# A four-layer graph network on one core: the mean of h from one product for four graphs, spread over the partitions by DMA

## The chip, the cores and the metric

The kernel runs on one core of one Trainium2 chip. The metric is the device time of one execution in microseconds (us), the median over runs of the same program. The engines are named as in the profile: PE is TensorE's matrix product, PEld its weight load, DVE is VectorE, ACT is ScalarE, POOL is GpSimd, and SP is SyncE, which here only issues DMAs.

## The reference

Sixteen graphs of 512 nodes with 128 features pass through four layers; each layer is a residual with a layer norm. The first three are attention layers with a dense 0/1 adjacency matrix. The first and the third take the softmax over a row:

```python
def layer0(x, adj_matrix, W, a):
    h = jnp.einsum('bnd,od->bno', x, W)
    e = (h @ a_left)[:, :, None] + (h @ a_right)[:, None, :]
    e = jnp.where(e > 0, e, LEAKY_SLOPE * e)
    e = jnp.where(adj_matrix == 0, NEG_INF, e)
    alpha = jax.nn.softmax(e, axis=-1)
    return jnp.einsum('bij,bjd->bid', alpha, h)
...
x = _layernorm(x + layer0(x, adj, ...), axis=-1)
x = _layernorm(x + layer1(x, adj, ...), axis=-1)   # softmax over the columns, then elu
x = _layernorm(x + layer2(x, adj, ...), axis=-1)   # as layer 0, with a bias in h, then elu
x = _layernorm(x + layer3(x, adj, ...), axis=-1)   # products with the relation masks
```

A row without an edge has all its scores at NEG_INF, so its softmax is uniform and its result is the mean of h over all 512 nodes. The kernel computes that mean for every graph of layers 0 and 2, and adds it in rows that are found to be empty.

## The kernel before, in words

All data stays in SBUF: X holds the 16 graphs (128 partitions, 4 chunks of 128 rows, 128 features), MT the masks. A work item is one graph in one layer; items 0 to 15 are layer 0, 16 to 31 layer 1, 32 to 47 layer 2, 48 to 63 layer 3. Every engine runs the same loop over slots n (`pipeline`), written out by hand: in slot n it treats the items at(-3) to at(4), that is n-3 to n+4, in an order fixed per engine, and waits for semaphores counted per item. No scheduler moves anything.

In slot n of layers 0 and 2:

- PE (from L495): transposes x of item n+4 into `xT_ps` (L416), spreads the column maximum of item n+2 (L459, `smax_ps`), spreads the row factors of item n+1 (L478), projects item n+3 (L437, `h_ps`; in layer 2 first two products that put the bias there, L432 and L434), multiplies the sum of x over the nodes, the same in every column, with the weights (L441, `h_mean_ps`, 128 x 128, so that the mean stands in every partition), and then attends for item n (L491).
- ACT (from L743): the node factors of item n+2, the scaled output of item n-3 (L706), then `take_h` of item n+3: `h_mean` out of PSUM (L643) and `hx` (L645); then xT of item n+4 (L634), with the sum of x over the nodes as accumulator output `x_sum`; in layer 0 also a check of the mask (L733).
- DVE (from L1033): sums of item n-1, the maximum of item n+2 (L897), then the output of item n-2 in layer 0 (y, L994) or of item n-1 in layer 2 (`lin`, which shares its space with `residual`, L994), then layer 2's elu (L1008) and the moments of item n-2, the weights PT of item n+1 (L942), and its own maximum of item n+3 (L892).
- POOL (from L306): scales h of item n+1 (L262). In layer 0 then `mean` of item n-1 (L238: `mean_term` = mean of h times the flag of empty rows) and the residual x + mean_term (L248). In layer 2 `mean` of item n+1, then the elu part of item n-1 (L287). Then 1/sqrt(variance) of item n-2 (L269, L272). In slots -4 to 7 POOL also issues the load of a mask (L225).
- SP: loads x graph by graph (L182), from graph 4 on held back until mask n-3 has landed, then the weights and bias of layer 3, then waits for the outputs (L195).

So in layer 0 the mean of item i is used by DVE in slot i+2 by way of the residual, in layer 2 in slot i+1 by `lin` itself. `mean_term` has two buffers. DVE's L994 waits for POOL's product, and POOL's product for ACT's `h_mean`.

Of the kernel before, what the change touches and what calls it, by code (L numbers as in the profile page):

```python
# [9 lines left out]
ACT = mybir.ActivationFunctionType  # L10
AX = mybir.AxisListType

P = 128
G = 16
N = 512
D = 128
# [17 lines left out]
class Item:  # L34


    def __init__(self, l, g, r):
        self.l, self.g, self.r, self.b, self.m = l, g, r % 4, r % 2, g % 8
        self.done = g + (G * l + 1)
        self.of_layer = g + 1  # L40


def item(n):
    return Item(n // G, n % G, n % G) if n >= 0 else None


def build(nc, x, adj, adj_rows, w_in, w_out, a_in, b2, ab2, w3, b3, out):
    ctx = ExitStack()
    with ctx:
        def sb(name, shape, dt=F32):  # L50
            return ctx.enter_context(nc.sbuf_tensor(name, shape, dt))
# [6 lines left out]
        def sem(name):  # L58
            if name not in sems:
                sems[name] = ctx.enter_context(nc.semaphore(name))  # L60
            return sems[name]


        X = sb("X", [P, G, C, D])
# [5 lines left out]
        empty_col = sb("empty_col", [P, G, C])  # L70
        x_cur = sb("x_cur", [P, C, D])
        xT = sb("xT", [P, 2, N])
        x_sum = sb("x_sum", [P, 2])
        hx = sb("hx", [P, 4, C, 132])
        h_mean = sb("h_mean", [P, 8, D])
        h_scaled = sb("h_scaled", [P, 2, C, 132])
# [35 lines left out]
        wx = sb("wx", [P, 3, 130])  # L112
# [24 lines left out]
        o_ps = [pb(f"o_ps{b}", [P, C, 256]) for b in range(2)]  # L137
        h_all_ps = h_ps[:, :, 0:260].rearrange("p k (c w) -> p k c w", c=2)
        smax_ps, h_mean_ps = h_ps[:, 0, 260:260 + P], h_ps[:, 1, 260:260 + D]

        def h_chunk_ps(c, width):

# [21 lines left out]
        def halves(it):  # L164

            return it.of_layer + (G if it.l == 2 else 0)
# [11 lines left out]
        @block.sync  # L178
        def _(sp):

            def load_x(it):
                sp.dma_start(X[:, it.g, :, :], x[it.g, :, :, :]).then_inc(sem(f"x_in{it.g}"), 16)  # L182

            for n in range(G):
                if n >= 4:

                    sp.wait_ge(sem(f"mask_in{n - 3}"), 16)
                load_x(item(n))
            sp.dma_start(w_rel[:, :, :], w3.rearrange("r d o -> d r o")).then_inc(sem("w_late"), 16)
            sp.dma_start(bias3[:, :], b3.partition_broadcast(P)).then_inc(sem("w_late"), 16)  # L190

            for n in range(G * LAYERS, G * (LAYERS + 1)):
                it = item(n)
                sp.wait_ge(sem("x_new"), it.done)
                sp.dma_start(out[it.g, :, :, :], X[:, it.g, :, :]).then_inc(sem("out"), 16)  # L195
            sp.wait_ge(sem("out"), 16 * G)

            with sp.If(not_binary(sp)):
                with sp.Fori(0, G) as g:
                    settle(sp)  # L200

                    sp.wait_ge(sem("re_adj_free"), g + 1)
                    sp.dma_start(adj_in[:, :, :], adj[g, :, :, :]).then_inc(sem("re_in"), 16)
                    sp.dma_start(X[:, g, :, :], x[g, :, :, :]).then_inc(sem("re_in"), 16)
                    sp.wait_ge(sem("re_x"), g * (LAYERS + 1) + (LAYERS + 1))
                    sp.dma_start(out[g, :, :, :], X[:, g, :, :]).then_inc(sem("re_out"), 16)
                sp.wait_ge(sem("re_out"), 16 * G)
# [4 lines left out]
        def _(pool):  # L212
# [14 lines left out]
            def mean(it):  # L227

                if it.l == 2:
                    if it.g >= 2:  # L230

                        pool.wait_ge(sem("y_lin"), it.of_layer - 2)
                elif it.g >= 2:
                    pool.wait_ge(sem("residual"), it.done - 2)
                pool.wait_ge(sem("h_mean"), halves(it))
                if it.l == 0:
                    pool.wait_ge(sem("empty_row"), it.of_layer)
                pool.tensor_tensor(mean_term[:, it.b, :, :],  # L238
                                   h_mean[:, it.m, :].unsqueeze(1).broadcast_to([P, C, D]),
                                   empty_row[:, it.g, :].unsqueeze(2).broadcast_to([P, C, D]),  # L240
                                   ALU.mult).then_inc(sem("mean_raw"), 1)

            def add_residual(it):
                if it.g >= 2:
                    pool.wait_ge(sem("y_sum"), it.done - 2)
                pool.wait_ge(sem(f"x_in{it.g}"), 16)
                pool.wait_ge(sem("mean_raw"), it.done)
                pool.tensor_tensor(residual[:, it.b, :, :], X[:, it.g, :, :], mean_term[:, it.b, :, :],  # L248
                                   ALU.add).then_inc(sem("residual"), 1)
# [56 lines left out]
            def attention_slot(at, n):  # L306
                if at(8) and at(8).l == 0:
                    load_mask(at(8))
                if at(1) and at(1).l != 1:
                    scale_h(at(1))  # L310
                if at(-1) and at(-1).l == 1:
                    elu_low(at(-1))
                if at(-1) and at(-1).l == 0:
                    mean(at(-1))
                    add_residual(at(-1))
                if at(1) and at(1).l == 2:
                    mean(at(1))
                if at(-1) and at(-1).l == 2:
                    elu_low(at(-1))
                if at(-2):  # L320
                    find_rstd(at(-2))
                if at(1) and at(1).l == 1:
                    scale_h(at(1))
                if n == G + 8:
                    split_bias2()
# [78 lines left out]
        def _(pe):  # L404
# [14 lines left out]
            def next_transpose(it):  # L419
                if it.l > 0 or it.g >= 1:  # L420

                    pe.wait_ge(sem("xT"), it.done - 1)
                if it.l == 0:
                    pe.wait_ge(sem(f"x_in{it.g}"), 16)
                else:
                    pe.wait_ge(sem("x_new"), it.done - G)
                transpose_x(X[:, it.g, :, :]).then_inc(sem("xT_ps"), 1)

            def project_layer(l, b):

                if l == 2:
                    pe.matmul(h_ps[:, 0, 0:260], rank_one[0:65, :], bias2_parts[0:65, 0:260],  # L432
                              start=True, stop=False)
                    pe.matmul(h_ps[:, 1, 0:260 + D], rank_one[0:65, :], bias2_parts[0:65, :],  # L434
                              start=True, stop=False)
                for c in range(C):
                    last = pe.matmul(h_chunk_ps(c, 130), xT[:, b, c * P:(c + 1) * P], wx[:, l, :],  # L437
                                     start=(l != 2), stop=(l != 2 or c == 1))
                if l in (0, 2):

                    last = pe.matmul(h_mean_ps, x_sum[:, b:b + 1].broadcast_to([P, P]), wx[:, l, 0:D],  # L441
                                     start=(l != 2), stop=True)
                return last

            def project(it):
                pe.wait_ge(sem("xT"), it.done)
                if it.l > 0 or it.g >= 1:

                    pe.wait_ge(sem("hx"), it.done - 1)
                    pe.wait_ge(sem("smax"), it.done - 1)  # L450
                if it.l == 2 and it.g == 0:
                    pe.wait_ge(sem("bias2_parts"), 1)
                last = project_layer(it.l, it.b)
                last.then_inc(sem("h_ps"), 1)

            def spread_max(it):
# [103 lines left out]
            def redo():  # L560
                with pe.Fori(0, G) as g:
                    for l in range(LAYERS):
# [2 lines left out]
                        transpose_x(x_cur).then_inc(sem("re_xT_ps"), 1)  # L565
                        pe.wait_ge(sem("re_xT"), g * (LAYERS + 1) + (l + 1))
                        last = project_layer(l, 0)
                        last.then_inc(sem("re_h_ps"), 1)
                        pe.wait_ge(sem("re_own"), k)
                        pe.transpose(smax_ps, smax_own[:, 0:1].broadcast_to([P, P]), ident[:])\  # L570
# [43 lines left out]
        def _(act):  # L614
# [13 lines left out]
            def take_xT(it):  # L628
                act.wait_ge(sem("xT_ps"), it.done)
                if it.l > 0 or it.g >= 2:  # L630

                    act.wait_ge(sem("h_ps"), it.done - 2)
                extra = dict(accum_out=x_sum[:, it.b:it.b + 1]) if it.l in (0, 2) else {}
                act.activation(xT[:, it.b, :], xT_ps[:], ACT.Copy, **extra).then_inc(sem("xT"), 1)  # L634

            def take_h(it):

                act.wait_ge(sem("h_ps"), it.done)
                if it.l in (0, 2):
                    if it.l > 0 or it.g >= 8:  # L640

                        act.wait_ge(sem("mean_raw"), halves(it) - 8)
                    act.activation(h_mean[:, it.m, :], h_mean_ps, ACT.Copy,  # L643
                                   scale=1.0 / N).then_inc(sem("h_mean"), 1)
                act.copy(halves_of(hx[:, it.r, :, 1:131]), h_all_ps).then_inc(sem("hx"), 1)  # L645

            def node_factors(it):
# [612 lines left out]
```

## Time and profile before

| What | us |
|---|---|
| median of 3 runs | 435.89 |
| lowest and highest run | 435.76 and 440.92 |
| profiled execution, its own time | 436.8 |
| span of its instructions | 435.0 |

The profile is of one execution of 436.8 us; 1.8 us of it lie around the span. Times of the trace count from the start of the span. Layer 0 begins some 27 us into the span with attention and ends at about 120 us, layer 1 ends at about 255 us, layer 2 at about 345 us, and layer 3 takes the rest. In timelines each row is a start, a duration, the engine, the line, the operation with what it writes and reads, and in brackets an idle time before it with the one who ended it.

### The profile page before, as it was taken

Reading aid. Unit: us, or ns where it says so; the run is one execution under the profiler, and the core shown is the slowest. Engines: PE = TensorE matmul, PEld = TensorE weight load, DVE = VectorE, ACT = ScalarE, POOL = GpSimd, SP = SyncE. Lnnn points to the kernel's source line nnn. Section 1 sums busy time; section 2 is a strip of 40 time slices with the busy share of each in tenths; the row PEclk is TensorE's granted clock in tenths of the full one; section 3 lists DMA queues with packets and bytes.
Section 4 is the critical chain, followed back from the end, with each engine's and each line's share of the span. In section 5 each row is a group of like instructions: output and inputs, shape, how many; then the busy total and the mean of one; then the engine's idle time right before and its main releaser. Section 6 shows DMA issues by size and latency. Waiting matters only on the chain. (4 is left out here: it accounts for less than half of the span.)

```text
span 435.0 us, 9097 instructions
## 1 busy us (share of the span) xinstructions
PE 364.8 (84%) x2781; PEld 322.5 (74%) x2781; DVE 367.5 (84%) x1406; ACT 301.4 (69%) x816; POOL 273.1 (63%) x335
## 2 busy tenths in 40 slices
PE   2689999999977797796878899999999779899950
PEld 1589999999966786685878899899898665554530
DVE  0077999999999999999999997999999988787861
ACT  1478999999755654645755677678777557777763
POOL 3326898777645543444453476787787846887882
PEclk9999999999989898989889899999999999999995
DMA  5999773000000000000000000000000000011222
GB/s 145 215 248 251 170 154 57 0 2 2 3 0 2 0 2 1 2 2 2 0 2 0 2 2 2 0 2 2 2 0 4 0 2 1 26 73 73 74 75 75
DMA packets 8755, 18.19 MB, mean 42 GB/s; under 512 B 1280, under 2 KB 2560, under 8 KB 8704
## 3 DMA queue, kind: packets, MB, share of 16 engines
q0 software_dynamic: 2304, 8.39, 10.3%
q1 hardware_dynamic: 5280, 8.72, 5.7%
q10 hardware_dynamic: 1120, 0.46, 0.5%
q8 instruction: 24, 0.39, 0.4%
q14 instruction: 27, 0.22, 0.2%
HBM read 21.76 MB, written 4.19 MB: 60 GB/s over the span
## 5 line engine op out<-in xcount | busy, mean ns | idle before, releaser
L491 PE MATMUL o_ps<-h_scaled,PT 128*128 128x129 f32 (+1 forms) x1536 | 190.4, 285 | 3.2 <-DVE PT L942 2.7
L491 PEld LDWEIGHTS o_ps<-h_scaled,PT 128*128 128x128 f32 x1536 | 185.8, 201 | 4.4 <-DVE PT L942 2.8
L942 DVE SCALAR_TENSOR_TENSOR PT<-rows_ps,factors,MT 128x512 f32<-128x512 f32 x128 | 88.8, 737 | 0.4
L706 ACT ACTIVATE X<-y,rstd 128x128 f32<-128x128 f32 x192 | 60.9, 389 | 23.2 <-POOL rstd L272 23.1
L437 PE MATMUL h_ps<-wx,xT 128*128 128x130 f32 x384 | 55.1, 288 | 26.0 <-DVE smax L897 25.4
L437 PEld LDWEIGHTS h_ps<-wx,xT 128*128 128x128 f32 x384 | 49.1, 196 | 32.8 <-issue 32.6
L272 POOL TENSOR_TENSOR rstd<-var_eps,neg_half 128x4 f32<-128x4 f32 x64 | 68.4, 1068 | 5.0
L1014 DVE BATCH_NORM_STATS2 stats<-y 128x6 f32<-128x128 f32 x256 | 56.0, 281 | 6.7 <-DVE y L994 0.5
L262 POOL TENSOR_TENSOR h_scaled<-hx,col_tmp 128x512 f32<-128x512 f32 x16 | 16.7, 1043 | 52.9 <-DVE col_tmp L962 52.9
L287 POOL TENSOR_TENSOR elu_exp<-elu_exp,X 128x512 f32<-128x512 f32 x32 | 40.7, 1273 | 13.3 <-ACT elu_exp L699 12.9
L238 POOL TENSOR_TENSOR mean_term<-h_mean,empty_row 128x512 f32<-128x512 f32 x32 | 38.1, 1192 | 14.5 <-DVE residual L994 14.0
L262 POOL TENSOR_TENSOR h_scaled<-hx,factors 128x516 f32<-128x516 f32 x32 | 35.1, 1096 | 18.9 <-PE o_ps L491 9.1
L937 DVE SCALAR_TENSOR_TENSOR PT<-MT,empty_col,edge 128x512 f32<-128x512 bf16 x64 | 44.3, 746 | 0.0
L920 DVE SCALAR_TENSOR_TENSOR edge<-q_rows,col_tmp,rows_ps 128x512 f32<-128x512 f32 x64 | 43.1, 737 | 0.2 <-ACT rows_ps L679 0.2
L712 ACT ACTIVATE X<-y,offset,rstd 128x128 f32<-128x128 f32 x64 | 26.4, 482 | 15.2 <-POOL offset L281 15.2
L269 POOL TENSOR_TENSOR var_eps<-mean_var,eps_tile 128x4 f32<-128x4 f32 x64 | 14.7, 230 | 32.4 <-DVE mean_var L1021 32.2
L416 PE MATMUL xT_ps<-ident,X 128*128 128x128 f32 x192 | 30.6, 284 | 4.7 <-ACT xT L634 4.3
L733 ACT ACTIVATE square_out<-MT,minus_half 128x2048 bf16<-128x2048 bf16 x16 | 32.0, 1999 | 0.0
L645 ACT COPY hx<-h_ps 128x520 f32<-128x520 f32 x48 | 27.8, 580 | 4.6 <-PE h_ps L437 4.3
L634 ACT ACTIVATE xT<-xT_ps 128x512 f32<-128x512 f32 x48 | 28.9, 601 | 1.3 <-PE xT_ps L416 1.3
L699 ACT ACTIVATE elu_exp<-elu_low_arg 128x512 f32<-128x512 f32 x32 | 20.2, 630 | 12.7 <-DVE y L1008 10.6
L416 PEld LDWEIGHTS xT_ps<-ident,X 128*128 128x128 f32 x192 | 22.7, 145 | 7.1 <-ACT xT L634 5.7
(112 smaller groups left out, 599.0 us busy)
## 6 DMA issues: line engine op xcount, KB each, us to landing
MT<-adj_by_j POOLq DMA_DIRECT2D x16, 512.0 KB, 9.6
X<-x SPq DMA_DIRECT2D x16, 256.0 KB, 6.3
out<-X SPq DMA_DIRECT2D x16, 256.0 KB, 2.0
w_rel<-w SPq DMA_DIRECT2D x1, 256.0 KB, 5.4
w_back<-w_by_output ACTq DMA_DIRECT2D x1, 192.0 KB, 3.4
wx<-w_by_input ACTq DMA_DIRECT2D x1, 192.0 KB, 6.3
bias<-b ACTq DMA_DIRECT2D x1, 64.0 KB, 5.0
bias<-b SPq DMA_DIRECT2D x1, 64.0 KB, 6.6
```

The source lines that it names most:

```text
L238: pool.tensor_tensor(mean_term[:, it.b, :, :], h_mean[:, it.m, :].unsqueeze(1).broadcast_to([P, C, D]), empty_row[:, it.g, :].unsqueeze(2) ...
L262: pool.tensor_tensor(h_scaled[:, it.b, :, first:1 + D], hx[:, it.r, :, first:1 + D], by.unsqueeze(2).broadcast_to([P, C, 1 + D - first]), ...
L272: pool.tensor_tensor(rstd[:, it.b, :], var_eps[:, it.b, :], neg_half[:], ALU.pow)\
L287: pool.tensor_tensor(elu_exp[:, :, :], elu_exp[:, :, :], X[:, it.g, :, :], ALU.add)\
L416: last = pe.transpose(xT_ps[:, c * P:(c + 1) * P], rows[:, c, :], ident[:])
L437: last = pe.matmul(h_chunk_ps(c, 130), xT[:, b, c * P:(c + 1) * P], wx[:, l, :], start=(l != 2), stop=(l != 2 or c == 1))
L491: last = pe.matmul(o_ps[it.b][:, ic, first:1 + D], PT[:, it.b, jc, ic * P:(ic + 1) * P], h_scaled[:, it.b, jc, first:1 + D], start=(jc == ...
L706: last = act.activation(X[:, it.g, c, :], y[:, it.b, c, :], ACT.Copy, scale=rstd[:, it.b, c:c + 1])
L920: dve.scalar_tensor_tensor(out=edge[:, c, :], in0=q_rows[:, :], scalar=col_tmp[:, it.b, WEIGHT, c:c + 1], in1=rows_ps[:], op0=ALU.mult, op ...
L937: dve.scalar_tensor_tensor(out=PT[:, it.b, c, :], in0=m, scalar=empty_col[:, it.g, c:c + 1], in1=edge[:, c, :], op0=ALU.max, op1=ALU.min, ...
L942: dve.scalar_tensor_tensor(out=PT[:, it.b, c, :], in0=rows_ps[:], scalar=factors[:, it.b, 1, c:c + 1], in1=m, op0=ALU.max, op1=ALU.mult, * ...
L1014: last = dve.bn_stats(stats[:, c, :], y[:, b, c, :])
```

## The change

The sums of x of four graphs are gathered in eight columns of `x_sum`. Once per four graphs, behind the projection of the last of them, PE multiplies these four columns with the weights, so that four means stand in four partitions (`group_mean_ps`). ACT copies these 4 x 128 numbers to `mean_rows`, and SP issues four DMAs, each of which reads one partition's 512 bytes 128 times and writes them to all partitions of one row of `h_mean`. POOL's `mean` waits for all four (`means_in`, counted to 64). In layer 2 `mean` now treats item n in slot n and comes behind the reciprocal root of item n-2. The 16 semaphores of x become four that are counted up, so SP waits for x of graph n-4 before it issues x of graph n. In layer 2 the bias of the means is a product of its own, once per four graphs, and the second bias product shrinks from 388 to 260 columns.

```diff
+        self.group = g // 4 + (G // 4 if l == 2 else 0)
...
-        x_sum = sb("x_sum", [P, 2])
+        x_sum = sb("x_sum", [P, 8])
+        mean_rows = sb("mean_rows", [P, 2, D])
...
+        group_mean_ps = h_ps[0:4, 1, 260:260 + D]
...
             def load_x(it):
-                sp.dma_start(X[:, it.g, :, :], x[it.g, :, :, :]).then_inc(sem(f"x_in{it.g}"), 16)
+                if it.g >= 4:
+                    sp.wait_ge(sem(f"x_in{it.r}"), 16 * (it.g // 4))
+                sp.dma_start(X[:, it.g, :, :], x[it.g, :, :, :]).then_inc(sem(f"x_in{it.r}"), 16)
+
+            def spread_means(group):
+
+                sp.wait_ge(sem("mean_rows"), group + 1)
+                if group >= 2:
+                    sp.wait_ge(sem("mean_raw"), 4 * (group - 1))
+                for k in range(4):
+                    m = 4 * (group % 2) + k
+                    sp.dma_start(h_mean[:, m, :], mean_rows[k:k + 1, group % 2, :].unsqueeze(1).broadcast_to([1, P, D]))\
+                        .then_inc(sem(f"means_in{group % 2}"), 16)
...
                 load_x(item(n))
+                if n in (6, 10, 14):
+                    spread_means((n - 6) // 4)
...
+            for group in range(3, 8):
+                spread_means(group)
...
-                pool.wait_ge(sem("h_mean"), halves(it))
+                pool.wait_ge(sem(f"means_in{it.group % 2}"), 64 * (it.group // 2 + 1))
...
-                if at(1) and at(1).l == 2:
-                    mean(at(1))
                 if at(-1) and at(-1).l == 2:
                     elu_low(at(-1))
                 if at(-2):
                     find_rstd(at(-2))
+                if at(0) and at(0).l == 2:
+                    mean(at(0))
...
-                    pe.matmul(h_ps[:, 1, 0:260 + D], rank_one[0:65, :], bias2_parts[0:65, :],
-                              start=True, stop=False)
+                    for k in range(2):
+                        pe.matmul(h_ps[:, k, 0:260], rank_one[0:65, :], bias2_parts[0:65, 0:260],
+                                  start=True, stop=False)
...
-                if l in (0, 2):
-
-                    last = pe.matmul(h_mean_ps, x_sum[:, b:b + 1].broadcast_to([P, P]), wx[:, l, 0:D],
-                                     start=(l != 2), stop=True)
                 return last
+
+            def project_sums(l, to, sums):
+
+                if l == 2:
+                    pe.matmul(to, rank_one[0:65, 0:to.shape[0]], bias2_parts[0:65, 260:260 + D], start=True, stop=False)
+                return pe.matmul(to, sums, wx[:, l, 0:D], start=(l != 2), stop=True)
...
+                if it.l in (0, 2) and it.g % 4 == 3:
+                    first = 4 * (it.group % 2)
+                    last = project_sums(it.l, group_mean_ps, x_sum[:, first:first + 4])
...
-                if it.l in (0, 2):
-                    if it.l > 0 or it.g >= 8:
-
-                        act.wait_ge(sem("mean_raw"), halves(it) - 8)
-                    act.activation(h_mean[:, it.m, :], h_mean_ps, ACT.Copy,
-                                   scale=1.0 / N).then_inc(sem("h_mean"), 1)
+                if it.l in (0, 2) and it.g % 4 == 3:
+                    if it.group >= 2:
+
+                        act.wait_ge(sem(f"means_in{it.group % 2}"), 64 * (it.group // 2))
+                    act.activation(mean_rows[0:4, it.group % 2, :], group_mean_ps, ACT.Copy,
+                                   scale=1.0 / N).then_inc(sem("mean_rows"), 1)
```

SP's queue, from its first instruction to the first output; X is the loaded x, `h_mean` the spread means. Before:

```order
L182 DMA X<-x 128x512 x16
L189 DMA w_rel<-w 128x4x128
L190 DMA bias<-b 128x128
L195 DMA out<-X 128x512 x16
L176 TENSOR_LOAD flag_int
```

The same stretch of SP's queue in the changed kernel:

```order
L187 DMA X<-x 128x512 x7
L196 DMA h_mean<-mean_rows 128x1x128 x4
L187 DMA X<-x 128x512 x4
L196 DMA h_mean<-mean_rows 128x1x128 x4
L187 DMA X<-x 128x512 x4
L196 DMA h_mean<-mean_rows 128x1x128 x4
L187 DMA X<-x 128x512
L206 DMA w_rel<-w 128x4x128
L207 DMA bias<-b 128x128
L196 DMA h_mean<-mean_rows 128x1x128 x20
```

Three groups of means now stand between loads of x; the other five follow the weights of layer 3.

POOL in one slot of layer 2, from one scaling of h to the next. Before:

```order
L262 TENSOR_TENSOR h_scaled<-hx,factors 128x4x129
L238 TENSOR_TENSOR mean_term<-h_mean,empty_row 128x512
L287 TENSOR_TENSOR elu_exp<-elu_exp,X 128x512
L269 TENSOR_TENSOR var_eps<-mean_var,eps_tile 128x4
L272 TENSOR_TENSOR rstd<-var_eps,neg_half 128x4
```

The same slot of POOL in the changed kernel:

```order
L282 TENSOR_TENSOR h_scaled<-hx,factors 128x4x129
L307 TENSOR_TENSOR elu_exp<-elu_exp,X 128x512
L289 TENSOR_TENSOR var_eps<-mean_var,eps_tile 128x4
L292 TENSOR_TENSOR rstd<-var_eps,neg_half 128x4
L258 TENSOR_TENSOR mean_term<-h_mean,empty_row 128x512
```

`mean_term` moved from second to last place in the slot, and it is one item later: that of the slot itself, which DVE reads in the next slot.

## Rows read from the trace of the kernel before

**Rows 1.** Busy time by engine, a stretch of layer 0 and of layer 2.
```profile
core 0: us, PE busy (x) PEld busy (x) DVE busy (x) ACT busy (x) POOL busy (x), PEclk, DMA share, GB/s
60.00:80.00 20.00, 19.88 (x172) 18.82 (x170) 18.54 (x93) 19.09 (x51) 16.71 (x19) 1.00 0.39 77
...
300.00:320.00 20.00, 19.77 (x163) 18.04 (x164) 18.12 (x64) 14.85 (x48) 15.18 (x16) 1.00 0.01 2
```

**Rows 2.** Timeline of PE and DVE in one slot of layer 0.
```profile
57.05 0.39 PE L441 MATMUL h_ps<-wx,x_sum 128*128 128x128 f32 x2
57.27 3.74 PE L491 MATMUL o_ps<-h_scaled,PT 128*128 128x129 f32 x32
...
55.64 0.29 DVE L897 TENSOR_REDUCE smax<-h_ps 128x1 f32<-128x128 f32 x1 [0.24 <-PE h_ps L459]
```

**Rows 3.** Timeline of two slots of layer 2, four engines, items 36 and 37.
```profile
284.76 0.25 ACT L643 ACTIVATE h_mean<-h_ps 128x128 f32<-128x128 f32 x1
...
287.65 1.13 DVE L994 SCALAR_TENSOR_TENSOR residual<-o_ps,rz_row,mean_term 128x128 f32<-128x128 f32 x4
...
288.69 0.68 DVE L1008 SCALAR_TENSOR_TENSOR y<-residual,elu_exp 128x512 f32<-128x512 f32 x1
...
288.86 1.42 POOL L238 TENSOR_TENSOR mean_term<-h_mean,empty_row 128x512 f32<-128x512 f32 x1 [1.05 <-DVE residual L994]
...
293.30 1.05 POOL L262 TENSOR_TENSOR h_scaled<-hx,factors 128x516 f32<-128x516 f32 x1
293.37 0.32 PE L459 MATMUL h_ps<-ident,smax_own 128*128 128x128 f32 x1
...
293.73 0.29 DVE L897 TENSOR_REDUCE smax<-h_ps 128x1 f32<-128x128 f32 x1 [0.35 <-PE h_ps L459]
...
294.19 1.13 DVE L994 SCALAR_TENSOR_TENSOR residual<-o_ps,rz_row,mean_term 128x128 f32<-128x128 f32 x4
```

**Rows 4.** DMA queue of SP, page part 3: packets, MB, share of 16 engines.
```profile
q1 hardware_dynamic: 5280, 8.72, 5.7%
```

**Rows 5.** The line that stores the outputs: issue time, time to landing.
```profile
L195 SPq DMA_DIRECT2D out<-X x16: 340/340/347, 376.0 to 430.6; - x16
...
DMA to landing us min/median/max: 2.0/2.0/2.8
```

**Rows 6.** Busy time by engine, while w_rel and while bias3 lands.
```profile
60.30:61.20 0.90, 0.90 (x11) 0.90 (x10) 0.90 (x6) 0.90 (x1) 0.90 (x2) 1.00 1.09 329
61.40:62.20 0.80, 0.76 (x7) 0.55 (x6) 0.61 (x4) 0.67 (x3) 0.77 (x2) 1.00 0.12 33
```

**Rows 7.** Timeline around the first slot of layer 2.
```profile
257.79 0.26 ACT L643 ACTIVATE h_mean<-h_ps 128x128 f32<-128x128 f32 x1
...
262.25 0.35 DVE L994 SCALAR_TENSOR_TENSOR residual<-o_ps,rz_row,mean_term 128x128 f32<-128x128 f32 x1 [0.44 <-issue]
```

**Rows 8.** Timeline of layer 0, items 4 to 7: ACT, POOL, DVE.
```profile
52.53 0.26 ACT L643 ACTIVATE h_mean<-h_ps 128x128 f32<-128x128 f32 x1
...
56.72 1.04 POOL L238 TENSOR_TENSOR mean_term<-h_mean,empty_row 128x512 f32<-128x512 f32 x1
57.93 1.28 POOL L248 TENSOR_TENSOR residual<-X,mean_term 128x512 f32<-128x512 f32 x1 [0.17 <-POOL mean_term L238]
...
61.88 1.10 DVE L994 SCALAR_TENSOR_TENSOR y<-o_ps,rz_row,residual 128x128 f32<-128x128 f32 x4
```

**Rows 9.** Timeline of the first slots of layer 0: ACT, DVE, PE.
```profile
27.51 0.28 ACT L643 ACTIVATE h_mean<-h_ps 128x128 f32<-128x128 f32 x1
...
38.08 1.13 DVE L994 SCALAR_TENSOR_TENSOR y<-o_ps,rz_row,residual 128x128 f32<-128x128 f32 x4
...
43.00 0.60 PE L416 MATMUL xT_ps<-ident,X 128*128 128x128 f32 x4
```

**Rows 10.** DMA issues between 27 and 29 us: KB, us from issue to landing.
```profile
X<-x SPq DMA_DIRECT2D x1, 256.0 KB, 9.1
```

More of the change, by code:

```diff
@@ L245, in add_residual @@
                     pool.wait_ge(sem("y_sum"), it.done - 2)
-                pool.wait_ge(sem(f"x_in{it.g}"), 16)
+                pool.wait_ge(sem(f"x_in{it.r}"), 16 * (it.g // 4 + 1))
                 pool.wait_ge(sem("mean_raw"), it.done)
@@ L423, in next_transpose @@
                 if it.l == 0:
-                    pe.wait_ge(sem(f"x_in{it.g}"), 16)
+                    pe.wait_ge(sem(f"x_in{it.r}"), 16 * (it.g // 4 + 1))
                 else:
@@ L431, in project_layer @@
                 if l == 2:
-                    pe.matmul(h_ps[:, 0, 0:260], rank_one[0:65, :], bias2_parts[0:65, 0:260],
-                              start=True, stop=False)
-                    pe.matmul(h_ps[:, 1, 0:260 + D], rank_one[0:65, :], bias2_parts[0:65, :],
-                              start=True, stop=False)
+                    for k in range(2):
+                        pe.matmul(h_ps[:, k, 0:260], rank_one[0:65, :], bias2_parts[0:65, 0:260],
+                                  start=True, stop=False)
                 for c in range(C):
                     last = pe.matmul(h_chunk_ps(c, 130), xT[:, b, c * P:(c + 1) * P], wx[:, l, :],
-                                     start=(l != 2), stop=(l != 2 or c == 1))
-                if l in (0, 2):
-                    last = pe.matmul(h_mean_ps, x_sum[:, b:b + 1].broadcast_to([P, P]), wx[:, l, 0:D],
-                                     start=(l != 2), stop=True)
-                return last
+                                     start=(l != 2), stop=(l != 2 or c % 2 == 1))
+                return last
+            def project_sums(l, to, sums):
+                if l == 2:
+                    pe.matmul(to, rank_one[0:65, 0:to.shape[0]], bias2_parts[0:65, 260:260 + D], start=True, stop=False)
+                return pe.matmul(to, sums, wx[:, l, 0:D], start=(l != 2), stop=True)
             def project(it):
@@ L567, in redo @@
                         last = project_layer(l, 0)
+                        if l != 1:
+                            last = project_sums(l, h_mean_ps, x_sum[:, 0:1].broadcast_to([P, P]))
                         last.then_inc(sem("re_h_ps"), 1)
@@ L632, in take_xT @@
                     act.wait_ge(sem("h_ps"), it.done - 2)
-                extra = dict(accum_out=x_sum[:, it.b:it.b + 1]) if it.l in (0, 2) else {}
+                extra = dict(accum_out=x_sum[:, it.m:it.m + 1]) if it.l in (0, 2) else {}
                 act.activation(xT[:, it.b, :], xT_ps[:], ACT.Copy, **extra).then_inc(sem("xT"), 1)
```

## The prediction

> **What bounds the kernel now.** I read the busy time by stretches first. In layer 0 PE is busy in 19.88 of 20 us and ACT in 19.09; in layer 2 PE again leads with 19.77, and DVE has 18.12 [rows 1]. A busy share alone doesn't say who sets the pace, so I then read a slot of each layer in order of time, and after that the DMA views, because the change puts DMAs between two engines that handed data to each other through SBUF.
>
> In layer 0 a slot lasts 5.95 us (y of item 0 starts at 38.08 [rows 9], of item 4 at 61.88 [rows 8]: 23.80 / 4). PE is full, and DVE stands idle 0.24 us per slot until PE has spread a maximum [rows 2]. So PE time that goes is time that comes back, up to about that 0.24 us, and not beyond, since DVE is bound right behind. In layer 2 a slot lasts 6.54 us (L994 at 287.65 and at 294.19) [rows 3]. There PE spreads the maximum (293.37) only when DVE has made its own maximum, and DVE's whole pause is 0.35 us until that small product comes back (293.73). The round runs over DVE, and a shorter PE does not shorten it.
>
> **What is removed.** A product with the sums takes PE 0.22 us until the next one starts (57.05 to 57.27) [rows 2]; twelve of sixteen go in each layer. Layer 0: 12 x 0.22 = 2.6 us, at best, which is also nearly all of DVE's pause. The first three graphs stand in a start-up where each step waits for the one before; I give them a product and ACT's copy of the mean (0.26) [rows 8]: 3 x 0.48 = 1.4 us. Layer 2: nothing, by the round above; the narrower bias product falls under the same answer. ACT's other copies are hidden by PE and DVE. Gain: 4.0 us.
>
> **What is added: a way of some microseconds between ACT and POOL.** Let L be the time from the end of ACT's copy of four means until POOL can start its product. It holds SP's wake-up and POOL's (0.05 us each, an estimate from hand-overs of 0.04 and 0.08 us: 293.69 to 293.73, 288.78 to 288.86 [rows 3]), what a DMA takes beside its data, and the data.
>
> A store of 256 KB lands 2.0 us after its issue [rows 5]. SP's queue moved 8.72 MB in 5.7% of 16 x 435.0 us = 397 us of engine time, 22 GB/s for one DMA engine [rows 4]. With 16 engines side by side 256 KB are 0.75 us, so 1.25 us lie beside the data. A group of means writes as much, 4 x 128 x 512 B = 262 KB, but it reads only four rows, each 128 times. No row shows an SBUF row read so often. Low end: as a store, 0.75 us of data. High end: all of it through one path at one engine's 22 GB/s, 11.9 us. The nearest row is bias3, also one row of 512 B copied to 128 partitions: while it lands, 33 GB/s flow at a DMA share of 0.12, and just before, with w_rel, 329 GB/s at 1.09 [rows 6]. The engines mostly wait for that one row. At 33 GB/s a group is 7.9 us. That source is in memory, not in SBUF, and four neighbouring partitions look to me more like one path, so I take the middle of 7.9 and 11.9: 9.9 us, L = 9.9 + 1.25 + 0.1 = 11.25 us.
>
> The Trainium skill, page "SBUF — State Buffer", section "Door 1: The DMA port swizzle", says that partitions 0 to 3 lie on one of 16 ports with about 27 GB/s, however many engines ask. The four rows of a group are just these partitions; by it the data would take an estimated 9.7 us, and the sum below would come out about 1.5 us lower. No run yet shows it.
>
> **Where the wait falls.** POOL's L238 waits for all four DMAs, and behind it in its queue stand the next scaling of h, the elu part and the reciprocal roots; DVE's L994 waits for L238, and behind that the whole round of DVE.
>
> *Layer 2.* Means of graphs 4 to 7 leave ACT at 284.76 + 0.25 = 285.01, and DVE wants the first of them at 287.65 [rows 3]: 2.64 us, less 1.04 for POOL's product [rows 8] and 0.07 for the hand-over, leave 1.53 us for L. The groups of graphs 8 to 11 and 12 to 15 stand alike. Graphs 0 to 3: 258.05 to 262.25 [rows 7], 4.20 - 1.11 = 3.09 us. Stall: 4 x 11.25 - 7.7 = 37.3 us. It isn't made up afterwards, because DVE itself is the round.
>
> *Layer 0.* Means of graphs 4 to 7 leave at 52.79; y of item 4 starts at 61.88 [rows 8]. POOL needs 1.21 from L238 to the start of L248, 1.28 for L248 and 0.07: 9.09 - 2.56 = 6.53 us for L. Stall 11.25 - 6.53 = 4.72, three groups 14.2 us.
>
> *The first group* leaves at 27.79 and y of item 0 starts at 38.08 [rows 9]: 10.29 - 2.56 = 7.73 us for L. But the masks fill the DMA engines: an x issued then lands after 9.1 us [rows 10], not 2.0, so up to 7.1 us come on top. POOL issues no mask while it waits, so the masks run out; I take half, L = 14.75, stall 7.0 us (3.5 to 10.6). x of graph 7 now stands behind these DMAs in SP's queue and would land near 27.8 + 14.75 + 2 = 45; PE takes it at 43.00 [rows 9] plus the stall, which hides it. If that cover went, 2 us.
>
> *The move of `mean` on POOL.* Where no DMA is awaited (12 slots of layer 2), it now starts where the scaling of h did, 293.30, ends 1.04 later, and with 0.07 DVE is served at 294.41 instead of 294.19 [rows 3]: 0.22 us, and since the reciprocal root waits for DVE, each slot: 2.6 us. In its old place it took 1.42 us beside DVE's L1008 [rows 3]; with that it would be 0.60 per slot, 7.2 us. The same page, section "Who interferes with whom", has POOL wait for a DVE instruction with two SBUF inputs, as L1008 is; in the new place stand only DVE steps with PSUM in them, so the rule leaves the 1.04. I take 1.04, the row of layer 0.
>
> *Nothing for the rest.* SP's extra waits ask for x of graph n-4, which was issued four loads earlier and lands within 9.1 us even under load [rows 10]; one that isn't over holds an x that PE takes only slots later, and costs at most those 9.1 us. ACT's wait for `means_in` two groups back is over by POOL's own wait.
>
> **Sum.** 37.3 + 14.2 + 7.0 + 2.6 - 4.0 = +57.1 us on the profiled execution's 436.8 us (span 435.0 and 1.8 around it): 493.9 us. The median of the runs is 0.9 us lower than that execution, so 493 to 494; I say 494. With 7.9 us of data (L = 9.25, first group 5.0): 29.3 + 8.2 + 5.0 + 2.6 - 4.0 = 41.1, 478 us. With 11.9 (L = 13.25, all 7.1 in the first group): 45.3 + 20.2 + 12.6 + 2.6 - 4.0 = 76.7, 513.5 us. That is the forecast's own range.
>
> **Rivals.**
>
> *Fast spread: not slower by what can be measured.* If the reads don't crowd, four issues of 0.34 us follow each other and the last lands 2.0 us later [rows 5]: L = 1.0 + 2.0 + 0.1 = 3.1. Layer 2: 12.4 - 7.7 = 4.7; layer 0 nothing; first group 3.1 + 7.1 - 7.7 = 2.5; the move 2.6; gain 4.0: +5.8, 442.6 us. It decides at an L of about 3.6, where the four groups of layer 2 have added 2 us more. For it: a store does it. Against it: bias3's 33 GB/s.
>
> *The waits vanish in slack I don't see*, and only the gain is left: 432.8 us. Against it: DVE's pause in layer 2 is 0.35 us per slot, with nothing to catch up from.
>
> *One engine alone carries a group.* 5280 packets in 397 us are 75 ns each [rows 4]; 512 packets on one engine 38.5 us, L = 40: 152 + 100 + 36 us, far over 700 us. For it: the source has one partition. Against it: the target has 128.
>
> *Pauses add more than themselves*, as where PE runs at a lower granted clock after them (now it is 1.00 in both stretches [rows 1]): above 514.
>
> **How the numbers follow.** Forecast (478 to 514) 0.70, fast spread 0.18, waits in slack 0.03, one engine 0.05, more than the pauses 0.04. A change of 2% is about what a measurement of this kernel can tell from none, 8.7 us. Fast spread lies within it with two thirds of its chance, 0.12, and with the slack case 0.15; faster 0.01; slower 0.84. The range holds the forecast's own and the fast case: 442 to 518.
>
> **What would show it.** Right: the issues of `h_mean` land 10 us or more after they are issued; POOL's L238 idles four times in layer 0 and four in layer 2, with a DMA as the one who ended it; DVE's L994 idles some 10 us four times in layer 2; the other slots of layer 2 take about 6.76 us. Wrong: landings of 2 to 3 us; four issues of one group that land evenly spaced by 2.5 us would be right, all at one time early would not. If the slots of layer 0 shrink by less than 0.2 us, the gain was over-read.

## The result and the profile after

| What | us |
|---|---|
| changed kernel, median of 4 runs | 514.94 (513.81 to 517.19) |
| kernel before, median of 4 runs beside it | 436.24 (435.76 to 440.92) |
| ratio, 95% interval | 1.1789 (1.171 to 1.1867) |
| span of the profiled execution | 513.3 (before 435.0) |

The change costs 78.7 us. The forecast was 494, its stated range 442 to 518, and the part of it that the forecast's own terms span ended at 514. The direction and the place of the waits came out; 21 us were missing in the sum.

The chain of waits first. In the page's line of the chain by engine, DMA comes second with 18%; in that by tile and line, the new DMA stands on top:

```profile
DVE 32%; DMA 18%; PE 14%; issue 12%; POOL 11%; ACT 8%; SPq 4%; DVEq 0%; ACTq 0%; POOLq 0%
DMA h_mean<-mean_rows 10%; PE o_ps L515 9%; DVE PT L963 8%; DVE edge L946 5%; DMA X<-x 5%; DVE stats L1040 5%; POOL rstd L292 3%; POOL mean_term L258 3%; SPq L196 3%; DVE residual L1020 3%; DVE y L1034 2%; ACT X L732 2%; DVE mean_var L1047 2%; PE h_ps L456 2%; ACT X L738 2%
```

The same page's queue of SP and its DMA issues (KB each, median us to landing), beside 5280 packets and 5.7% in [rows 4]:

```profile
q1 hardware_dynamic: 9888, 10.82, 14.3%
...
out<-X SPq DMA_DIRECT2D x16, 256.0 KB, 2.0
h_mean<-mean_rows SPq DMA_DIRECT2D x32, 64.0 KB, 8.6
```

That is 4608 packets more, and 64 KB of means take 8.6 us (the median of the 32) where 256 KB of output take 2.0.

Who waited for whom, from the view of the waits (us in total, times, longest):

```profile
POOL mean_term L258 <- DMA h_mean<-mean_rows: 67.1, 7, 10.9
...
DVE residual L1020 <- POOL mean_term L258: 45.8, 14, 10.6
...
PE o_ps L515 <- DVE y L1020: 24.4, 5, 7.1
DVE y L1020 <- POOL residual L268: 23.8, 4, 7.1
```

Seven times POOL's product waits for the DMA (an eighth, 9.9 us, is put down to "issue"); four of these eight pass to DVE's y in layer 0, four to `residual` in layer 2. One such place in layer 2, from the timelines of ACT, POOL and DVE, beside [rows 3]:

```profile
290.49 0.27 ACT L669 ACTIVATE mean_rows<-h_ps 4x128 f32<-4x128 f32 x1
...
302.71 1.04 POOL L258 TENSOR_TENSOR mean_term<-h_mean,empty_row 128x512 f32<-128x512 f32 x1 [10.91 <-DMA h_mean<-mean_rows]
...
304.24 1.13 DVE L1020 SCALAR_TENSOR_TENSOR residual<-o_ps,rz_row,mean_term 128x128 f32<-128x128 f32 x4 [9.05 <-POOL mean_term L258]
```

ACT's copy ends at 290.76 and POOL starts at 302.71: L is 11.95 us (forecast 11.25). The other three waits of DVE for a group in layer 2 are 10.65, 10.64 and 10.46 us; with this one, 40.8. The other 5.0 of the 45.8 us are short waits for the moved `mean`.

One place in layer 0, DVE and PE:

```profile
77.08 1.13 DVE L1020 SCALAR_TENSOR_TENSOR y<-o_ps,rz_row,residual 128x128 f32<-128x128 f32 x4 [7.06 <-POOL residual L268]
...
84.87 0.16 DVE L993 TENSOR_SCALAR empty_row<-o_ps 128x4 f32<-128x4 f32 x1 [2.13 <-PE o_ps L515]
```
```profile
65.25 3.81 PE L515 MATMUL o_ps<-h_scaled,PT 128*128 128x129 f32 x32
...
78.35 6.49 PE L515 MATMUL o_ps<-h_scaled,PT 128*128 128x129 f32 x32 [7.14 <-DVE y L1020]
```

DVE waits 7.06 us, PE behind it 7.14, and then the attention itself takes 6.49 us instead of 3.81, for which DVE waits another 2.13. The granted clock around this pause (stretch, its length, PE busy, PEclk, DMA share, GB/s):

```profile
63.00:71.00 8.00, 7.92 (x68) 1.00 0.78 59
71.20:74.00 2.80, 0.01 (x1) 0.94 1.03 322
74.00:78.20 4.20, 0.00 (x0) 0.50 0.26 97
78.40:80.50 2.10, 2.10 (x10) 0.50 0.39 39
80.50:83.00 2.50, 2.50 (x14) 0.50 0.90 180
83.00:84.60 1.60, 1.60 (x12) 0.71 0.00 0
85.00:91.00 6.00, 5.96 (x52) 1.00 0.46 84
```

In the pause the clock falls to 0.50 (1.2 GHz), the first 4.6 us of the attention run at that, it rises within the last 1.6 us (0.71 on the mean), and the next slot runs at 1.00 (2.4 GHz). The prediction had this as a rival of its own with a chance of 0.04, not as a term.

### The profile page after: what moved, and what is told of

Same layout as the page of the kernel before. It is cut to its first block, busy times and chain, and to the rows that moved or that the text cites. A ratio compares the mean times of both kernels' runs of the same rounds, so it can differ in the third digit from the quotient of the medians.

```text
span 513.3 us, 9010 instructions
## 1 busy us (share of the span) xinstructions
PE 376.4 (73%) x2730; PEld 332.1 (65%) x2737; DVE 369.4 (72%) x1406; ACT 297.8 (58%) x792; POOL 268.7 (52%) x335
## 4 chain that ended last, share of the span: by engine, by line
DVE 32%; DMA 18%; PE 14%; issue 12%; POOL 11%; ACT 8%; SPq 4%; DVEq 0%; ACTq 0%; POOLq 0%
DMA h_mean<-mean_rows 10%; PE o_ps L515 9%; DVE PT L963 8%; DVE edge L946 5%; DMA X<-x 5%; DVE stats L1040 5%; POOL rstd L292 3%; POOL mean_term L258 3%; SPq L196 3%; DVE residual L1020 3%; DVE y L1034 2%; ACT X L732 2%; DVE mean_var L1047 2%; PE h_ps L456 2%; ACT X L738 2%
## 5 line engine op out<-in xcount | busy, mean ns | idle before, releaser
L515 PE MATMUL o_ps<-h_scaled,PT 128*128 128x129 f32 (+1 forms) x1536 | 200.4, 294 | 26.5 <-DVE y L1020 24.4
L515 PEld LDWEIGHTS o_ps<-h_scaled,PT 128*128 128x128 f32 x1536 | 195.1, 210 | 30.3 <-issue 27.0
L456 PE MATMUL h_ps<-wx,xT 128*128 128x130 f32 x384 | 58.9, 302 | 26.4 <-DVE smax L923 25.7
L258 POOL TENSOR_TENSOR mean_term<-h_mean,empty_row 128x512 f32<-128x512 f32 x32 | 35.7, 1115 | 78.2 <-DMA h_mean<-mean_rows 67.1
L456 PEld LDWEIGHTS h_ps<-wx,xT 128*128 128x128 f32 x384 | 52.0, 209 | 33.3 <-issue 32.9
L307 POOL TENSOR_TENSOR elu_exp<-elu_exp,X 128x512 f32<-128x512 f32 x32 | 40.8, 1273 | 34.3 <-ACT elu_exp L725 34.3
L1020 DVE SCALAR_TENSOR_TENSOR residual<-o_ps,rz_row,mean_term 128x128 f32<-128x128 f32 x64 | 18.0, 345 | 45.9 <-POOL mean_term L258 45.8
L282 POOL TENSOR_TENSOR h_scaled<-hx,factors 128x516 f32<-128x516 f32 x32 | 33.6, 1050 | 22.0 <-PE o_ps L515 13.9
L719 ACT ACTIVATE elu_low_arg<-residual 128x512 f32<-128x512 f32 x16 | 10.1, 630 | 52.1 <-DVE residual L1020 51.8
L675 ACT ACTIVATE shifts<-shift_k,smax 128x3 f32<-128x3 f32 x32 | 9.4, 295 | 46.9 <-DVE smax L923 46.9
L1020 DVE SCALAR_TENSOR_TENSOR y<-o_ps,rz_row,residual 128x128 f32<-128x128 f32 x64 | 17.7, 340 | 23.8 <-POOL residual L268 23.8
```

What stands on the lines that cost most here:

```text
L258: pool.tensor_tensor(mean_term[:, it.b, :, :], h_mean[:, it.m, :].unsqueeze(1).broadcast_to([P, C, D]), empty_row[:, it.g, :].unsqueeze(2) ...
L282: pool.tensor_tensor(h_scaled[:, it.b, :, first:1 + D], hx[:, it.r, :, first:1 + D], by.unsqueeze(2).broadcast_to([P, C, 1 + D - first]), ...
L515: last = pe.matmul(o_ps[it.b][:, ic, first:1 + D], PT[:, it.b, jc, ic * P:(ic + 1) * P], h_scaled[:, it.b, jc, first:1 + D], start=(jc == ...
L1020: last = dve.scalar_tensor_tensor(out=to[:, it.b, c, :], in0=o[:, c, 1:1 + D], scalar=rz_row[:, it.b, c:c + 1], in1=add[:, it.b, c, :], op ...
```

## The experiments

Times of before beside them were 436.05 to 436.42 us.

**Which layer loses what.** Two kernels keep the change in one layer (`GROUPED` is (0,) in the first, (2,) in the second) and the single means of before in the other; `mean` on POOL stands in layer 2 where each needs it:

```diff
+GROUPED = (0,)
-                if it.l in (0, 2) and it.g % 4 == 3:
+                if it.l in (0, 2) and it.l not in GROUPED:
+                    last = project_sums(it.l, h_mean_ps, x_sum[:, it.m:it.m + 1].broadcast_to([P, P]))
+                if it.l in GROUPED and it.g % 4 == 3:
```

> The change in layer 0 alone; layer 2 has a product and a copy for each graph as before. The theory that the wait for the four DMAs costs in both layers, with slower products of PE after each pause in layer 0: 23.8 us of DVE's waits for the residual and four times 2.4 us behind them, +33, about 469 us. Without the slower products +24, 460. Rival, layer 2 carries nearly all: below 445.

> The change in layer 2 alone; layer 0 as before. The wait theory: four waits of 10.6 us at most (42 us), and 12 slots at 0.27 us (3 us): +45, 481 us; with the layer 0 run the two excesses add up to 78 us. Rival, the layers share a cost (a slower clock over the whole run, or x arriving late): the excesses add up to less than 65 us.

Layer 0 alone: 469.55 us, ratio 1.0767 (1.073 to 1.0803), +33.2. Layer 2 alone: 481.35 us, 1.1036 (1.1009 to 1.1062), +45.0. Both are as expected. The sum, 78.2, is the whole loss within the spread of the runs, so the two can be treated apart.

**What a spread costs.** Behind the last output of the kernel before, where the DMA engines have nothing else to do, SP issues copies within SBUF that nobody reads, each kind after the landing of the one ahead. It was run once, and only its landings are read:

```diff
+            def spread(p, row):
+                sp.dma_start(edge[:, row, 0:D], X[p:p + 1, 0, 0, :].unsqueeze(1).broadcast_to([1, P, D]))\
+                    .then_inc(sem("out"), 16)
+            spread(0, 0)
...
+            for k in range(4):
+                spread(k, k)
...
+            for k in range(4):
+                spread(4 * k, k)
...
+                sp.dma_start(edge[:, k, 0:D], X[:, 2, k, :]).then_inc(sem("out"), 16)
```

> The kernel before, with DMAs within SBUF behind its last output that nothing reads, so only their landings count, each step waiting for the one before. Theory A (the path of the source partition limits): a row of 512 B to 128 partitions lands 4.6 us after its issue (2.0 beside the data, 2.6 of data), four from partitions 0 to 3 take 12 us in all, one DMA of 2 KB pieces from one partition (256 KB, 128 pieces) as much, 11 to 12 us; four DMAs in which each partition reads its own row (the same bytes and pieces) only 3 to 4 us. Theory B (512 small pieces limit, wherever they come from): the 2 KB pieces need 4 to 5 us, the four plain ones 12 us. Theory C (a fixed cost for each DMA limits): 2 KB pieces 4.6 us, plain ones 12 us. Four rows in partitions 0, 4, 8 and 12 on one queue: under A between 4.5 us (the engines run ahead to the next row) and 12 us (they work through one row at a time). Two queues, two rows each: from partitions 0 to 3 under A again 12 us, from 0, 4, 8, 12 down to 7 us.

Three windows of the DMA issues (the one row; the last of four rows from partitions 0 to 3; the last of four from 0, 4, 8, 12; KB, us to landing):

```profile
edge<-X SPq DMA_DIRECT2D x1, 64.0 KB, 4.0
...
edge<-X SPq DMA_DIRECT2D x1, 64.0 KB, 9.9
...
edge<-X SPq DMA_DIRECT2D x1, 64.0 KB, 4.9
```

From the first issue to the last landing, one row takes 4.0 us, four neighbours 11.67, four rows apart 6.7, and four copies of 128 different rows 3.8. The neighbours land 2.57, 2.55 and 2.00 us apart: 65.5 KB in 2.57 us are 25 GB/s. One DMA of 2 KB pieces from one partition (256 KB in all) took 11.1 us as well, so neither the number of DMAs nor the 512 bytes set it. Each of the four apart still takes 3.7 to 4.9 us, about as long as one row alone, but they run side by side. With two of the four issued by ACT, the neighbours took 11.2 us, near the expected 12, and the four apart 5.1, less than the expected 7. The stretches of the neighbours and of the four apart, by windows (no engine is busy; PEclk, DMA share, GB/s at the end):

```profile
437.00:448.00 11.00, 0.00 (x0) 0.00 (x0) 0.00 (x0) 0.00 (x0) 0.00 (x0) 0.50 0.61 24
448.50:454.80 6.30, 0.00 (x0) 0.00 (x0) 0.00 (x0) 0.00 (x0) 0.00 (x0) 0.50 0.53 42
```

Ten engines' worth of time (0.61 of 16) moves 24 GB/s. That reads as engines that count as busy while they queue at the source; no view shows the queue itself. The Trainium skill, page "SBUF — State Buffer", section "Door 1: The DMA port swizzle", puts partitions 0 to 3 on one port of about 27 GB/s and partitions 0, 4, 8 and 12 on four; the measured 25 GB/s and the gain from the distance agree with it.

**The same in the kernel.** The changed kernel with its four means in partitions 0, 4, 8, 12:

```diff
-        group_mean_ps = h_ps[0:4, 1, 260:260 + D]
+        group_mean_ps = h_ps[0:13, 1, 260:260 + D]
-                    sp.dma_start(h_mean[:, m, :], mean_rows[k:k + 1, group % 2, :].unsqueeze(1).broadcast_to([1, P, D]))\
+                    sp.dma_start(h_mean[:, m, :], mean_rows[4 * k:4 * k + 1, group % 2, :].unsqueeze(1).broadcast_to([1, P, D]))\
-                    last = project_sums(it.l, group_mean_ps, x_sum[:, first:first + 4])
+                    last = project_sums(it.l, group_mean_ps, x_sum[:, first:first + 13])
```

> The changed kernel with the four mean rows in partitions 0, 4, 8 and 12 instead of 0 to 3; sizes, number of DMAs and order stay. Theory A (the four neighbouring source partitions share one path): issue to last landing falls from 11.7 to 6.7 us as it did behind the last output, L from 12 to 7. Layer 2: four waits shorter by 5.0, -20 us. Layer 0: the four waits of 5.2 to 7.1 us fall to 0.2 to 2.1, -20 us, and the slow attention behind them mostly goes, up to -8 more. 467 to 475 us. Rival B (512 bytes per descriptor, or the number of DMAs, sets the time): landings of a group stay 2.6 us apart, 515 us.

479.11 us, ratio 1.0941 (1.0881 to 1.1001): 36 us back, 4 short of the nearer expected end. A group of layer 2, the DMA's stretch and the waits:

```profile
306.90:313.60 6.70, 6.61 (x58) 6.05 (x57) 2.24 (x11) 2.46 (x10) 1.28 (x3) 1.00 0.48 42
```
```profile
DVE residual L1021 <- POOL mean_term L258: 25.8, 15, 5.4
...
PE o_ps L515 <- DVE y L1021: 9.6, 2, 5.9
DVE y L1021 <- POOL residual L268: 9.4, 2, 5.8
```

42 GB/s as behind the output; DVE's waits in layer 2 fall from 45.8 to 25.8 us, just the expected 20. In layer 0 two of four waits are gone; the first two (5.83 and 3.62 us) stand under the loads of masks and x, and their attentions still take 6.39 and 6.58 us. So theory A, the path that neighbouring source partitions share, holds; the 4 us that are short of it lie in layer 0's first two groups.

**The clock behind a pause.** The changed kernel, with products nobody reads while PE waits for y:

```diff
+                if it.l == 0 and it.g % 4 == 2:
+                    pe.wait_ge(sem("z_row"), it.of_layer - 1)
+                    for k in range(22):
+                        pe.matmul(o_ps[1 - it.b][:, 0, 130:256], ident[:], ident[:, 0:126], start=True, stop=True)
```

> The changed kernel, and in the four pauses of layer 0 PE computes 22 products nobody reads, while it waits for y (some 5 us; nothing else of the work differs). Theory: the 2 to 2.7 us by which the attention behind such a pause is longer than 3.8 us come from the pause itself (a lower granted clock after PE stood idle), and they are on the path: attention behind the pauses returns to some 3.8 us, four times 2 to 2.7 us less, 505 to 507 us. Rival 1: the slow products are there but cost nothing, because DVE or ACT has to catch up anyway: attention returns to 3.8, time stays at 515. Rival 2: they are slow for another reason (late inputs): attention stays at 5.5 to 6.5 us, time 515 or above.

504.77 us, ratio 1.1563 (1.1505 to 1.1622): 10.2 us less, where 8 to 10 were expected. PE and DVE of this run at the second pause; then the granted clock over the stretch 61.00 to 94.50, of the changed kernel and then of this one:

```profile
67.69 5.07 PE L512 MATMUL o_ps<-ident 128*128 128x126 f32 x44
73.18 3.84 PE L519 MATMUL o_ps<-h_scaled,PT 128*128 128x129 f32 x32 [0.42 <-DVE y L1024]
```
```profile
72.00 1.13 DVE L1024 SCALAR_TENSOR_TENSOR y<-o_ps,rz_row,residual 128x128 f32<-128x128 f32 x4 [5.34 <-POOL residual L268]
```
```profile
61.00:94.50 33.50, 26.21 (x198) 24.59 (x197) 22.36 (x109) 22.25 (x62) 20.11 (x24) 0.85 0.53 90
```
```profile
61.00:94.50 33.50, 32.87 (x276) 30.86 (x276) 26.35 (x124) 26.39 (x74) 19.54 (x23) 1.00 0.60 91
```

The attentions behind the four pauses take 3.84 us each instead of 6.24, 6.49, 5.84 and 5.53, and the clock is at 1.00. The four slots behind the pauses, from y to y, are 24.65 us together instead of 32.68, so the slowness came from the pause and 8.0 us of it lay on the path. Most of the other 2 us aren't the clock's: DVE waits 1.7 us less for the second group (5.34 against 7.06), whose DMAs are done 12.0 us after the first issue here and 13.8 in the changed kernel, both under the loads of masks and x. In layer 2 the clock falls to 0.50 as well (302.60 to 306.00), but little of it shows on the path: from stall to stall (304.24 to 341.28) are 37.04 us, of which 10.65 are the wait and 26.39 four slots, against 4 x 6.54 = 26.16 before, and that holds the moved mean too. No run changes the clock there alone.

**The gain alone.** The kernel before with product and copy only for every fourth graph; the means of the other graphs are left out (zero):

```diff
-                if l in (0, 2):
+                if with_sums:
...
-                last = project_layer(it.l, it.b)
+                last = project_layer(it.l, it.b, it.l in (0, 2) and it.g % 4 == 3)
...
-                if it.l in (0, 2):
+                if it.l in (0, 2) and it.g % 4 == 3:
```

> The kernel before with the product of the sums and ACT's copy of the mean only for every fourth graph; the means of the other graphs are left out (they count as zero). It shows the gain alone, without the DMAs. Theory of the prediction: 3 x 0.48 in the start-up, 12 x 0.22 in layer 0, nothing in layer 2: -4.0, 432.3 us. Rival, from the trace of the changed kernel (undisturbed slots of layer 0 are 5.92 us there against 5.95): PE's attention waits for y of the item before the last, which DVE sets, so 12 x 0.03 and at most the start-up's 1.4: -0.4 to -1.8, 434.5 to 436 us.

436.05 us, ratio 0.9981 (0.9959 to 1.0004): 0.4 us, no difference that can be told. The timelines of PE and of DVE in a slot of layer 0 (its projection and attention; the maximum and y):

```profile
60.97 1.13 PE L442 MATMUL h_ps<-wx,xT 128*128 128x130 f32 x8
62.07 3.81 PE L496 MATMUL o_ps<-h_scaled,PT 128*128 128x129 f32 x32
```
```profile
60.53 0.29 DVE L902 TENSOR_REDUCE smax<-h_ps 128x1 f32<-128x128 f32 x1 [0.22 <-PE h_ps L464]
...
60.83 1.10 DVE L999 SCALAR_TENSOR_TENSOR y<-o_ps,rz_row,residual 128x128 f32<-128x128 f32 x4
```

The product with the sums is gone, yet the attention can't start before 62.07, 0.14 us after y ends at 61.93: the attention of item n writes the PSUM buffer that y of item n-2 reads, and `attend` waits for `y_sum`. In the kernel before, y of the same slot ended at 61.88 + 1.10 = 62.98 [rows 8], and the attention started at 63.22, 0.24 us behind it, with the product between:

```profile
63.00 0.39 PE L441 MATMUL h_ps<-wx,x_sum 128*128 128x128 f32 x2
63.22 3.74 PE L491 MATMUL o_ps<-h_scaled,PT 128*128 128x129 f32 x32
```

So 0.10 of the 0.22 us was to be had, and 0.07 of it goes again in the attention, 3.81 us instead of 3.74 [rows 2]. A slot takes 5.93 us against 5.95. The round is PE's attention, transposes and spread, DVE's maximum and y, and PE's attention again; most of the product stood in the shadow of y.

**The move of the mean on POOL.** The kernel before with `mean` in its new place and nothing else:

```diff
-                if at(1) and at(1).l == 2:
-                    mean(at(1))
...
+                if at(0) and at(0).l == 2:
+                    mean(at(0))
```

> The kernel before with one part of the change: in layer 2 POOL's product of the mean treats item n in slot n, behind the reciprocal root; means come from PE as before. My step: 0.22 us in each slot, here 15 slots without a DMA to wait for, so +3.3 us, 439 to 440 us. Rival, the product keeps its 1.42 us: 0.60 per slot, +9 us, 445. Rival, slack hides it: 436.

442.57 us, ratio 1.0146 (1.0121 to 1.0171): +6.2, more than the expected 3.3 and less than the rival's 9. A slot's end on POOL, and DVE:

```profile
300.20 0.20 POOL L269 TENSOR_TENSOR var_eps<-mean_var,eps_tile 128x4 f32<-128x4 f32 x1 [0.45 <-DVE mean_var L1021]
300.48 1.02 POOL L272 TENSOR_TENSOR rstd<-var_eps,neg_half 128x4 f32<-128x4 f32 x1
301.47 1.04 POOL L238 TENSOR_TENSOR mean_term<-h_mean,empty_row 128x512 f32<-128x512 f32 x1
```
```profile
302.64 1.13 DVE L994 SCALAR_TENSOR_TENSOR residual<-o_ps,rz_row,mean_term 128x128 f32<-128x128 f32 x4 [0.37 <-POOL mean_term L238]
```

The mean takes 1.04 us there, as forecast, and the slot 6.81 us (295.83 to 302.64) against 6.54: +0.27, where 0.22 was forecast. That is 2.5 us in the nine slots from 268.57 to 329.91. The last slots of layer 2, beside the start of layer 3, cost more, 7.82 us (352.04 to 359.86) against 7.17, and the last `residual` of layer 2 is 5.8 us late (366.62 against 360.84).

**x's semaphores in turn.** The kernel before with these alone:

```diff
+                if it.g >= 4:
+                    sp.wait_ge(sem(f"x_in{it.r}"), 16 * (it.g // 4))
```

> The kernel before with x's semaphores in turn and nothing else of the change. Theory (the prediction's): x of graph n-4 has long landed when SP asks for it, so no change, 436 us (within 1). Rival: part of what layer 0 lost (33 us) comes from SP's waits, which hold x back behind loads under the masks' traffic; then 440 us or more, and PE would wait for x at its transposes.

436.51 us, ratio 0.9997 (0.9974 to 1.0021): nothing, as forecast.

**With a source that doesn't crowd.** The changed kernel, with 128 different rows as the source of each DMA; the means themselves are left out:

```diff
-                    sp.dma_start(h_mean[:, m, :], mean_rows[k:k + 1, group % 2, :].unsqueeze(1).broadcast_to([1, P, D]))\
+                    sp.dma_start(h_mean[:, m, :], ident[:, 0:D])\
```

> The changed kernel, but each of the four DMAs of a group copies 128 different rows of 512 bytes (of the identity, each to its own partition) instead of one row 128 times. Sizes, number, order and waits stay; the means themselves are left out. It shows what the change costs when the source doesn't crowd, the prediction's fast rival. Behind the last output four such copies took 3.8 us in all, so L is some 4.1. Layer 2: 4 x 4.1 - 7.7 = 8.7 us of stall and 4.2 for the move of the mean on POOL (as in the run with that move alone, 4 to 6); layer 0: no stall but the first groups' under the mask loads, up to 3.5; gain 0.4. 449 to 453 us: still slower than before. Rival 1: the count of descriptors sets the time, not the source: 515. Rival 2: the prediction's fast case with its gain of 4.0: 442.6.

459.01 us, ratio 1.0512 (1.0483 to 1.0542), 6 us above the expected range. From the views of the waits and of POOL and DVE:

```profile
DVE residual L1020 <- POOL mean_term L258: 15.2, 15, 2.6
...
DVE y L1020 <- POOL residual L268: 5.0, 2, 3.9
```
```profile
300.18 1.04 POOL L258 TENSOR_TENSOR mean_term<-h_mean,empty_row 128x512 f32<-128x512 f32 x1 [2.16 <-DMA h_mean<-ident]
```

Layer 2 is as expected: ACT's copy ended at 296.24, L is 3.94 us, DVE waits 2.56 there. Layer 0 was underrated: by y of item 14 it is 8.9 us behind (133.38 against 124.53), of which two waits make 5.0, an attention of 5.45 us behind the first makes 1.6, and three slots in which a group's product stands 0.3 each (6.23 us, 56.77 to 63.00); the other 1.4 stand ahead of layer 0's first attention (28.81 against 27.31), and their cause stays open. So even a spread without crowding makes the kernel slower by 5%; the other 56 us of the changed kernel come with the crowded source, and not with the count of descriptors, which is the same here.

## Why the prediction was right, and where it was short

| Term | forecast, us | measured, us | from |
|---|---|---|---|
| layer 2, four waits | 37.3 | 40.8 | the rows of `residual` |
| layer 0, groups 1 to 3 | 14.2 | 17.5 | 7.06 + 5.25 + 5.20 |
| first group | 7.0 | 6.3 | wait of DVE's first y |
| move of the mean | 2.6 | 4.2 | a remainder: 45.0 of layer 2 alone less 40.8 |
| slower attention behind the pauses | none | 8.0 | 32.68 - 24.65, the slots with and without products nobody reads |
| gain | -4.0 | -0.4 | products left out |
| sum | +57.1 | +76.4 | +78.7 measured |

Of the 2.3 us that the rows leave, three slots with a group's product make 0.9; the rest stays open. The remainder in the row of the move holds whatever else layer 2 gained or lost; alone, in all slots of layer 2, the move cost 6.2.

*The range: kept by its margin.* The forecast's own terms ended at 513.5, and the result lies above, where the prediction had put its rival of the slower clock at 0.04. The 4 us from 514 to 518 belong to no term, so that the time is still inside is luck. The mechanism of the waits isn't luck: most of the signs that it named came, eight waits of POOL for the DMAs, four of DVE of 9.1 to 10.7 us in layer 2, landings 2.0 to 2.6 us apart and slots of 6.82 us between the stalls. Not each DMA of a group lands 10 us after its own issue, as the sign had it; in most groups only the last does, and the first lands after 4.6.

*The data of a group: the size right, partly by luck.* The first of the four DMAs of the group copied at 290.49 landed 4.6 us after its issue at 290.78, the others 2.6, 2.6 and 2.0 us behind one another. With 64 KB of different rows landing in 1.9 us, that leaves some 10 us of data. But 9.9 was the middle between a row in memory and one DMA engine's mean rate, and neither is the path that set the pace.

*Beside the data: mis-sized.* The step "so 1.25 us lie beside the data" took 0.75 off a landing of 2.0. With the 0.1 of wake-ups, L - 9.9 was to be 1.35; it is 2.05. That 0.7 in each of seven groups makes 4.9 of the 6.8 us that the first two terms lack. The rest is in the second group of layer 0, which stands under the traffic of masks and x: 13.9 us from ACT's copy to POOL (60.57 to 74.48).

*The gain: the step that failed.* "So PE time that goes is time that comes back" read the pace from a full PE and a short pause of DVE. The slot was a round over both engines, joined where PE writes the PSUM buffer that y has read, and the product stood where PE would have waited for y. The start-up's 1.4 us can't be told either: with the products left out y of item 0 starts at 37.06 instead of 38.08, but in the runs that keep layer 0 as before it starts at 37.30 and 37.34. In the changed kernel a slot with a group's product even takes 6.24 us (57.77 to 64.01 for DVE's y): the product with four columns holds PE 0.31 us, from 58.98 to the attention at 59.29.

*The clock: a rival that belonged into the sum.* The forecast had pauses of 5 to 7 us for PE in layer 0, where PE sits in the round, so each had to be priced with the attention behind it. It gave 8.0 us of the 21 that were short. In layer 2, where PE has slack, the four slots from one stall to the next are only 0.2 us longer than before.

*The move: the place right, the ends not.* 0.27 instead of 0.22 in the middle; 0.65 in the slots that share DVE and POOL with layer 3, which the forecast priced as the others.

*The fast rival* (442.6) is refuted twice: the spread is not fast, and with a fast one the kernel takes 459, because the gain isn't there, L is 3.94 us instead of 3.1, and waits in layer 0 remain.

## What to carry to other kernels

A broadcast from one row by DMA was limited here at the place it reads from (4.0 us, against 1.9 for as many bytes from 128 rows): count the bytes read from the source's partitions, not only those written, and put several source rows on partitions some way apart (here 4 apart: 11.7 to 6.7 us). Before pricing a saved instruction on a full engine, look at what the instruction behind it waits for: if that ends at the same moment, the saved time is only a wait. And a stall put into a round with PE is to be priced with the slower matmuls behind it.

No version tried beats the kernel before: with the products left out and no spread at all the saving is 0.4 us, too small to tell from none, and with the cheapest spread tried, the moved mean included, the kernel is 23 us slower.

## What the runs showed of the hardware that was not expected

The share of busy DMA engines says nothing of progress here: at 0.61 they moved 24 GB/s from one group of four partitions, while before the change 1.09 went with 329 GB/s [rows 6], and bias3's 0.12 with 33. The forecast took bias3's low share as the mark of a crowded row; a crowded row in SBUF shows a high one.

A pause of PE of 7.1 us made the 32 products behind it 2.7 us longer at a granted clock of 0.50, and 5.07 us of products that nobody reads, in the same place, gave all of it back. Work thrown away cost nothing here, since it stood in a wait.
